# Two layers of message passing on one core: a prologue in two halves, and another order of the last steps of layer 0

## The chip, the core and the metric

The kernel runs on one core of one Trainium2 chip. The metric is the time of one launch in microseconds (us), taken on the device; three runs of the kernel before gave 2295.61, 2296.75 and 2296.79, a median of 2296.75. The core has five engines that run beside each other: TensorE (PE; PEld are its weight loads), VectorE (DVE), ScalarE (ACT), GpSimd (POOL) and SyncE (SP), and DMA queues that SP, ACT and POOL feed (SPq, ACTq, POOLq). Engines wait for each other by semaphores.

## The reference

N = 6250 nodes of D = 128 numbers and E = 106250 edges, sorted by destination.

```
h = relu(layernorm(x))
# layer 0: edge softmax per channel
msg = h[src] + edge_attr;  s = msg * beta
e = exp(s - segment_max(s, dst)[dst])
agg = segment_sum(msg * e / segment_sum(e)[dst], dst)
x = x + (agg @ H + bias + h)             # H from phm_rule and W
h = relu(layernorm(x))
# layer 1: graph attention, 4 heads of 32
Wx = h @ W.T;  logits = leaky_relu(a1.Wx[src] + a2.Wx[dst])
x = x + elu(segment_sum(softmax_per_dst(logits) * Wx[src], dst))
```

## The kernel before, in words

Edges are taken in groups of 512 (GE), four blocks of 128 (GB = 4); there are NG = 208 groups. Nodes are 49 tiles of 128 rows, in 13 batches of four tiles (the last has one). All inputs of x stay in SBUF as `nodes`.

Prologue. SyncE loads x in six parts of 512 KB and a small tail, then the weights. VectorE measures all 49 tiles (`statistics`, L869) and works out all norms at once (`norm_all_nodes`, L878 to L890: 18 small operations, each waiting for the one before). ScalarE loads the lists: src, dst and `prev` (dst shifted by one edge), eight of its eleven DMAs for the last two. When the norms are there, ScalarE makes h = relu(norm(x)) for the even batches (L673, a tile at a time) and VectorE for the odd ones (L912 four tiles, L916 the maximum of the batch). SyncE stores h batch by batch into `h_dram` (L381, L383), in order of batches. GpSimd adds h to `nodes` for even batches as they come (`even_residual`, L563), VectorE for odd ones after its list work (L941). List work: VectorE casts src (L904) and dst (L922), compares dst with prev to get run flags (L924, L925), TensorE transposes the tables (L1190), ScalarE copies them to `meta` (L687, L690), and SyncE brings the first lists to `meta_g` (L441 for src, L453 for the keys). Then follow packed offsets (L948 to L951), the matrix H (L957, L959) and constants on VectorE.

Layer 0 is one loop on each engine, `sweep_edges`, each engine with its own stages and lags; a stage at lag n handles group g - n in step g. GpSimd gathers four times 128 rows of h for each group (L582), waiting for the list, for h_stored, and for the lift of group g - 4. ScalarE lifts the rows to PSUM (`lift0`, L749, into row_psum), VectorE adds edge_attr (`add0`, L1017) and makes the one-hot (L1043), TensorE turns (`turn0`, L1238), VectorE scans for segment maxima in both directions and works out the drop between groups (`maxima0`, L994, L999, L1006, which counts `dropped`), TensorE turns back and subtracts (`unturn0`, L1245, L1249, into bank 2), ScalarE takes Exp twice (`weigh0`, L732, L735, L737), VectorE multiplies (`products0`, L1029), TensorE sums into `own_sums` (`sums0`, L1229), ScalarE merges that into the accumulator `acc` (`merge0`, L711 to L719). The loops run over their last steps in the same order as over the others; only before the last merge ScalarE loads the table of Ln (L752). After its last gather GpSimd adds the bias to all 13 batches of `nodes` (`add_bias`, L595).

Middle stage: ScalarE takes Ln and Exp (L760, L767), GpSimd multiplies (L606, L608), VectorE (L1059) and TensorE (L1272) finish layer 0, VectorE adds to `nodes` (L1068) where `bias_added` has come, measures and norms again. Layer 1 is a second loop of the same make; its last steps are written out by hand with `last(stage, back)`, which runs a stage for group NG - 1 - back, and use `spare_sums` in turn with `own_sums`. The order of instructions on each engine is the order of the program; there is no planner.

Of the kernel before, what the change touches and what calls it, by code (L numbers as in the profile page):

```python
# [70 lines left out]
def gnn_kernel(nc, x_in, src_in, dst_in, ea_in, rule_in, w0_in, bias_in, beta_in, w1_in, a_in, out):  # L71
# [31 lines left out]
    with ctx:  # L103
# [104 lines left out]
        row_psum = sums[:, 1, 0, :]  # L208
# [5 lines left out]
        own_sums, spare_sums = sums[:, 0, :, :], banks[:, 0:2, :]  # L214
# [40 lines left out]
        h_even = sem("h_even")  # L255
        h_odd = sem("h_odd")
        even_sum = sem("even_sum")
        odd_sum = sem("odd_sum")
        h_stored = sem("h_stored")
        bias_added = sem("bias_added")  # L260
# [64 lines left out]

        def extent(b):
            return (1, LAST) if b == NBAT - 1 else (GB, P)
# [16 lines left out]
        def _(sp):  # L344
# [12 lines left out]
            for i in range(PH):  # L357
# [16 lines left out]
            def store_h(b):  # L374
                t, r = extent(b)
                if b % 2:
                    sp.wait_ge(h_odd, b // 2 + 1)
                else:
                    sp.wait_ge(h_even, b // 2 + 1)
                if t == 1:  # L380
                    sp.dma_start(h_dram[b * GE:N, :], h_rows[0:r, b, 0, :]).then_inc(h_stored, 16)  # L381
                else:
                    sp.dma_start(h_dram[b * GE:(b + 1) * GE, :].rearrange("(t p) d -> p t d", p=P), h_rows[:, b, :, :]  # L383
                                 ).then_inc(h_stored, 16)

            straight(NBAT, [(0, store_h)])
# [131 lines left out]
        def _(pool):  # L518
# [39 lines left out]
            def even_residual(b):  # L558
                if b % 2 == 0:
                    t, r = extent(b)  # L560
                    pool.wait_ge(h_even, b // 2 + 1)
                    tiles = nodes[:, b * GB:b * GB + t, :]
                    pool.tensor_tensor(tiles, tiles, h_rows[:, b, 0:t, :], ALU.add).then_inc(even_sum, 1)  # L563

            straight(NBAT, [(0, even_residual)])
# [22 lines left out]
            pool.wait_ge(even_sum, (NBAT + 1) // 2)  # L588
            pool.wait_ge(odd_sum, NBAT // 2)
            pool.wait_ge(weights_in, 16 * W_DMA)  # L590

            def add_bias(b):
                t = 1 if b == NBAT - 1 else GB
                tiles = nodes[:, b * GB:b * GB + t, :]
                pool.tensor_tensor(tiles, tiles, bias_all[:, :].rearrange("p (a d) -> p a d", a=1).to_broadcast([P, t, D]),  # L595
                                   ALU.add).then_inc(bias_added, 1)

            straight(NBAT, [(0, add_bias)])
# [38 lines left out]
        def _(act):  # L637
# [7 lines left out]
            def load_list(flat, tile, done):  # L645
# [8 lines left out]
            act.wait_ge(x_loaded[4], 16)  # L654
            load_list(dst_in, dst_i, dst_in_sbuf)
            act.dma_start(prev_i[0:1, 0, 1:P], dst_in[0:P - 1].rearrange("(a e) -> a e", a=1)).then_inc(prev_in_sbuf, 16)
            act.dma_start(prev_i[1:P, 0, :], rows(dst_in, P - 1, P - 1)).then_inc(prev_in_sbuf, 16)
            act.dma_start(prev_i[:, 1:ct, :], dst_in[P * P - 1:ct * P * P - 1].rearrange("(t c e) -> c t e", c=P, e=P)
                          ).then_inc(prev_in_sbuf, 16)
            act.dma_start(prev_i[0:tail, ct, :], rows(dst_in, ct * P * P - 1, tail)).then_inc(prev_in_sbuf, 16)  # L660
            act.dma_start(prev_i[tail:tail + 1, ct, 0:E - FULL * P + 1],
                          dst_in[FULL * P - 1:E].rearrange("(a e) -> a e", a=1)).then_inc(prev_in_sbuf, 16)
# [3 lines left out]
            act.wait_ge(normed, 1)  # L666

            def even_h(b):
                if b % 2 == 0:
                    t, r = extent(b)  # L670
                    for i in range(t):
                        n = b * GB + i
                        ins = act.activation(h_rows[:, b, i, :], nodes[:, n, :], ACT.Relu,  # L673
                                             bias=norm[:, 1, n:n + 1], scale=norm[:, 0, n:n + 1])
                    ins.then_inc(h_even, 1)

            straight(NBAT, [(0, even_h)])
# [45 lines left out]
            act.wait_ge(blk_loaded, 16)  # L723

            act.wait_ge(h_stored, 16 * NBAT)
            act.wait_ge(even_sum, (NBAT + 1) // 2)

            def weigh0(g, s, use):
# [3 lines left out]
                act.activation(wgt[:, s % WGT, :, :], bank[2][:, :].rearrange("p (b d) -> p b d", b=GB), ACT.Exp)  # L732
                if later(g, 1):
                    act.wait_ge(L0["multiplied"], g)
                act.activation(wgt_psum, bank[2][:, :], ACT.Exp).then_inc(L0["weighed"], 1)  # L735
# [3 lines left out]
            def merge0(g, s, use):  # L739
                if isinstance(g, int) and g == 0:  # L740
                    act.wait_ge(odd_sum, NBAT // 2)
                merge(g, s, use, L0, None)
# [8 lines left out]
            sweep_edges(act, [(5, merge0), (0, lift0), (3, weigh0)], until=NG + 4)  # L751
# [39 lines left out]
            act.wait_ge(normed, 2)  # L791
# [61 lines left out]
        def _(dve):  # L853
# [21 lines left out]
            def norm_all_nodes():  # L875
                y, t, v = norm[:, 0, :], newton[:, :], spread_v[:, :]

                link(dve.tensor_tensor(t, stats[:, :, 1], stats[:, :, 4], ALU.subtract))  # L878
                link(dve.scalar_tensor_tensor(y, t, 0.25, t, ALU.mult, ALU.mult))
                link(dve.tensor_tensor(v, stats[:, :, 2], stats[:, :, 5], ALU.add))  # L880
                link(dve.scalar_tensor_tensor(v, v, 1.0 / D, y, ALU.mult, ALU.add))
                link(dve.tensor_tensor(mean_2[:, :], stats[:, :, 1], stats[:, :, 4], ALU.add))
# [7 lines left out]
                dve.scalar_tensor_tensor(norm[:, 1, :], mean_2[:, :], -0.5, y, ALU.mult, ALU.mult).then_inc(normed, 1)  # L890
# [3 lines left out]
            for k in range(LDX - 1):  # L894
# [6 lines left out]
            norm_all_nodes()  # L901

            dve.wait_ge(src_in_sbuf, 48)
# [281 lines left out]
        def _(pe):  # L1185
# [67 lines left out]
            def sums0(g, s, use):  # L1253
                segment_sums(g, s, L0)
# [137 lines left out]
```

## Time and profile before

| | |
|---|---|
| median of three runs | 2296.75 us |
| the profiled execution | 2297.38 us, its span 2295.6 us |
| PE, PEld busy | 88%, 79% |
| DVE busy | 87% |
| ACT busy | 59% |
| POOL busy | 72% |
| granted TensorE clock, mean | 0.945 |

Times in the views count from the start of the span. A busy share is an average over stages; the chain of waits goes back from the last instruction to what released each step, and tells which work ended last. "issue" in it is time in which an engine waited for nothing that the profile shows. Rows of a timeline give start, length, engine, line and operation, output<-input, shape and the number of instructions merged, and in brackets the idle time before with what ended it. A row of several instructions spans from the start of the first to the end of the last.

### The profile page before, as it was taken

What the parts mean: (1) busy time and instruction counts of PE and PEld (TensorE: products, weight loads), DVE (VectorE), ACT (ScalarE), POOL (GpSimd) and SP (SyncE); (2) the same over time, 40 slices, a digit from 0 to 9 for tenths busy, and PEclk for the clock granted to TensorE, in tenths of its full rate; (3) what the DMA queues carried; (4) which work ended last, traced back from release to release, by engine and by line L of the source; (5) the groups of instructions that cost most, each with busy time, mean ns of one, the idle gap of its engine ahead of it and who ended that gap; (6) DMA issues with size and microseconds to landing.
All of it is one profiled execution on the core that took longest, in us unless ns stands there. A gap on an engine that the chain in (4) does not pass through costs nothing.

```text
span 2295.6 us, 63252 instructions
## 1 busy us (share of the span) xinstructions
PE 2013.3 (88%) x15341; PEld 1806.1 (79%) x15342; DVE 1997.8 (87%) x3846; ACT 1361.5 (59%) x3479; POOL 1648.3 (72%) x1741
## 2 busy tenths in 40 slices
PE   1899999999999999998458999999999999999996
PEld 0778887888887888787458888888888888888885
DVE  7888989898989998999477888888888888888887
ACT  2566666666666666666544555555555555555555
POOL 4777777777777777777427777777777777777772
PEclk9999999999999999999677999999999999999998
DMA  7444454444444444443023333333333333333322
GB/s 209 116 132 135 131 136 131 126 131 135 131 136 131 136 129 128 131 136 99 1 62 61 61 58 59 58 59 59 59 59 59 58 59 59 58 59 58 59 60 67
DMA packets 338046, 214.22 MB, mean 93 GB/s; under 512 B 169981, under 2 KB 304502, under 8 KB 337990
## 3 DMA queue, kind: packets, MB, share of 16 engines
q0 software_dynamic: 53248, 112.57, 20.0%
q1 hardware_dynamic: 282190, 99.72, 17.3%
q10 hardware_dynamic: 2552, 1.28, 0.2%
q8 instruction: 24, 0.39, 0.1%
q14 instruction: 32, 0.26, 0.0%
HBM read 201.37 MB, written 10.29 MB: 92 GB/s over the span
## 4 chain that ended last, share of the span: by engine, by line
POOL 43%; issue 20%; DMA 14%; DVE 10%; PE 6%; ACT 4%; SPq 1%; POOLq 0%; ACTq 0%; DVEq 0%
POOL msg L618 23%; POOL ring_h L582 19%; DMA ring_h<-h_dram,meta_g 11%; PE sums L1229 3%; DVE sums L994 2%; DMA msg<-wx_dram,meta_g 2%; DVE seg_max L999 2%; ACT sums L749 2%; DVE onehot L978 1%; DVE prod L1129 1%; ACT acc L719 1%; PE banks L1238 1%; POOL ring_h L608 1%; PE banks L1245 1%; POOL diff L606 1%
## 5 line engine op out<-in xcount | busy, mean ns | idle before, releaser
L618 POOL DMA_INDIRECT msg<-wx_dram,meta_g x832 | 791.9, 952 | 293.5 <-issue 246.3
L582 POOL DMA_INDIRECT ring_h<-h_dram,meta_g x832 | 788.6, 948 | 260.8 <-issue 248.7
L1229 PE MATMUL sums<-onehot,prod 128*128 128x128 f32 x3312 | 688.2, 291 | 15.1 <-issue 6.1
L1229 PE MATMUL sums<-onehot,wgt 128*128 128x128 f32 x3312 | 674.1, 287 | 0.0
L1229 PEld LDWEIGHTS sums<-onehot,prod 128*128 128x128 f32 x3312 | 535.8, 204 | 47.7 <-issue 47.2
L1229 PEld LDWEIGHTS sums<-onehot,wgt 128*128 128x128 f32 x3312 | 536.7, 204 | 0.0
L719 ACT ACTIVATE acc<-sums 128x1022 f32 x412 | 422.0, 1024 | 0.2
L1238 PE MATMUL banks<-beta_ident,msg 128*128 128x128 f32 x1664 | 243.5, 290 | 91.3 <-DVE msg L1017 89.9
L749 ACT ACTIVATE sums<-ring_h 128x512 f32<-128x512 f32 x208 | 125.1, 602 | 321.7 <-DMA ring_h<-h_dram,meta_g 321.7
L1238 PEld LDWEIGHTS banks<-beta_ident,msg 128*128 128x128 f32 x1664 | 204.8, 194 | 119.7 <-issue 92.8
L1249 PEld LDWEIGHTS banks<-neg_ident,seg_max 128*128 128x128 f32 x1664 | 219.6, 192 | 100.5 <-issue 100.0
L994 DVE TENSOR_TENSOR_SCAN sums<-flags,seg_max,banks 4x512 f32<-4x512 bf16 x207 | 264.0, 1275 | 6.2 <-PE banks L1325 4.5
L994 DVE TENSOR_TENSOR_SCAN banks<-flags,seg_max,banks 128x512 f32<-128x512 bf16 x207 | 264.9, 1280 | 0.0
L999 DVE TENSOR_TENSOR_SCAN seg_max<-flags,banks 128x512 f32<-128x512 bf16 x208 | 253.9, 1220 | 7.2
L999 DVE TENSOR_TENSOR_SCAN seg_max<-flags,sums 4x512 f32<-4x512 bf16 x208 | 251.1, 1207 | 7.2
L711 ACT ACTIVATE carried<-acc,scale 128x2 f32 x414 | 121.5, 294 | 206.0 <-PE sums L1229 181.6
L1017 DVE TENSOR_TENSOR msg<-msg,sums 128x512 f32<-128x512 f32 x208 | 143.0, 687 | 89.8 <-ACT sums L749 82.7
L1249 PE MATMUL banks<-neg_ident,seg_max 128*128 128x128 f32 x1664 | 220.2, 275 | 0.0
L1316 PEld LDWEIGHTS banks<-window,onehotT 128*128 128x128 f32 x1664 | 211.6, 199 | 9.4 <-issue 8.1
L1245 PE MATMUL banks<-msg,beta_ident 128*128 128x512 f32 x416 | 214.8, 598 | 0.2 <-ACT sums L735 0.2
L1316 PE MATMUL banks<-window,onehotT 128*128 128x4 f32 x1664 | 205.8, 247 | 8.5 <-DMA window<-wx_dram 7.3
L808 ACT ACTIVATE sums<-logit_d 128x16 f32<-128x16 f32 x208 | 39.1, 188 | 256.3 <-DVE logit_d L1121 254.0
(162 smaller groups left out, 2806.3 us busy)
## 6 DMA issues: line engine op xcount, KB each, us to landing
msg<-in_edge_attr SPq DMA_DIRECT2D x207, 256.0 KB
flags<-flag_dram SPq DMA_DIRECT2D x52, 512.2 KB
ring_h<-h_dram,meta_g POOLq DMA_INDIRECT x832
msg<-wx_dram,meta_g POOLq DMA_INDIRECT x832
window<-wx_dram SPq DMA_DIRECT2D x832, 2.0 KB
wx_dram<-msg SPq DMA_DIRECT2D x13, 272.0 KB, 2.4
nodes<-in_x SPq DMA_DIRECT2D x6, 512.0 KB, 6.8
h_dram<-acc SPq DMA_DIRECT2D x12, 256.0 KB
```

The source lines that it names most:

```text
L582: pool.indirect_dma_start(hg[:, s % HRING, b, :], None, h_dram, bass.IndirectOffsetOnAxis(ap=meta_g[:, s, b:b + 1], axis=0)).then_inc(L0[" ...
L618: pool.indirect_dma_start(msg[:, s, b, :], None, wx_dram, bass.IndirectOffsetOnAxis(ap=meta_g[:, s, b:b + 1], axis=0)).then_inc(L1["gather ...
L719: act.activation(acc[:, :, bass.ds(node + 1, WIN - 1)], where[:, :, 1:WIN], ACT.Copy).then_inc(k["merged"], 1)
L749: act.activation(row_psum, ring_h[:, s % HRING, :], ACT.Copy).then_inc(L0["lifted"], 1)
L994: dve.tensor_tensor_scan(run, flag[:, 0:GE], data, before, ALU.add, ALU.max).then_inc(k["scanned"], 1)
L999: dve.tensor_tensor_scan(seg_max[0:n, par, ::-1], flag[:, GE:0:-1], run[:, ::-1], -BIG, ALU.add, ALU.max).then_inc(k["scanned"], 1)
L1017: dve.tensor_tensor(msg[:, s, :, 0:D], msg[:, s, :, 0:D], row_psum.rearrange("p (b d) -> p b d", b=GB), ALU.add).then_inc(L0["added"], 1)
L1229: ins = pe.matmul(where[:, j, bass.ds(off, P)], what[:, slot, b, :], onehot[:, s, b, :], start=(b == 0), stop=(b == GB - 1), skip_group_ch ...
L1238: ins = pe.matmul(bank[s % 2][:, b * P:(b + 1) * P], msg[:, s, b, 0:D], beta_ident[:, :], start=True, stop=True)
L1245: pe.matmul(bank[2][:, :].rearrange("p (b d) -> p b d", b=GB), beta_ident[:, :], msg[:, s, :, 0:D], start=True, stop=False, skip_group_che ...
L1249: ins = pe.matmul(bank[2][:, b * P:(b + 1) * P], seg_max[:, s % 2, b * P:(b + 1) * P], neg_ident[:, :], start=False, stop=(b == GB - 1), s ...
L1316: ins = pe.matmul(bank[1][:, b * H:(b + 1) * H], onehotT[:, s % 2, b * P:(b + 1) * P], window[:, s, b, :], start=True, stop=True)
```

## The change

- The two PSUM banks of `row_psum` and of the shift (the output of `unturn0`) change places; `spare_sums0` is banks 2 and 3. TensorE writes zeros to bank 3 once at the start.
- Prologue: `norm_nodes(lo, hi)` takes the place of `norm_all_nodes`. VectorE measures three parts of x (24 tiles, six batches), works out their norms, casts src, measures the rest and works out its norms. ScalarE makes h for batches 0 to 5, copies the src table, then makes h for 6, 8, 10 and 12; VectorE makes 7, 9 and 11. SyncE stores batches 0 to 5 in between the weights, the others in the order 7, 6, 9, 8, 11, 10, 12. The eight DMAs for dst and prev are issued by GpSimd, when the last full part of x has landed. GpSimd adds h to `nodes` for batches 0, 2 and 4, after VectorE's three batches; VectorE for the other ten.
- Bias: even batches on GpSimd, once all of layer 0's drops are made; odd ones on VectorE behind its last product.
- Last steps of layer 0: written out by hand on ScalarE, VectorE and TensorE, as in layer 1, with the spare banks for groups 204 and 206.

```diff
-        row_psum = sums[:, 1, 0, :]
+        shift_psum = sums[:, 1, 0, :]
+        row_psum = bank[2]
+        spare_sums0, spare_sums = banks[:, 2:4, :], banks[:, 0:2, :]
+        FRONT = 6
+        BY_DVE = (7, 9, 11)
+        BY_ACT = tuple(b for b in range(NBAT) if b not in BY_DVE)
+        POOL_SUMS = (0, 2, 4)
+        DVE_SUMS = tuple(b for b in range(NBAT) if b not in POOL_SUMS)
 # sync
             for i in range(PH):
+                store_h(i)
                 (rule_rep and w0_rep as before)
             for h in range(H):
+                if h < FRONT - PH:
+                    store_h(PH + h)
                 (a_col as before)
             (wx_dram pads as before)
-            straight(NBAT, [(0, store_h)])
+            for b in (7, 6, 9, 8, 11, 10, 12):
+                store_h(b)
 # gpsimd
-            straight(NBAT, [(0, even_residual)])
+            pool.wait_ge(x_loaded[5], 16)
+            pool.dma_start(dst_i[:, 0:ct, :], ...)        # 3 for dst_i, 5 for prev_i, which ACT issued before
...
+            pool.wait_ge(h_dve, len(BY_DVE))
+            for b in POOL_SUMS:
+                wait_row_batch(pool, b)
+                tiles = nodes[:, b * GB:(b + 1) * GB, :]
+                pool.tensor_tensor(tiles, tiles, h_rows[:, b, :, :], ALU.add).then_inc(pool_sum, 1)
             pool.wait_ge(h_stored, 16 * NBAT)
 (after the gathers of layer 0)
-            straight(NBAT, [(0, add_bias)])
+            pool.wait_ge(L0["dropped"], NG)
+            straight(NBAT, [(0, even_bias)])
 # scalar
+            act.wait_ge(normed, 1)
+            for b in range(FRONT):
+                h_by_act(b)
             (src table)
+            act.wait_ge(normed, 2)
+            for b in BY_ACT[FRONT:]:
+                h_by_act(b)
-            sweep_edges(act, [(5, merge0), (0, lift0), (3, weigh0)], until=NG + 4)
+            sweep_edges(act, [(5, merge0), (0, lift0), (3, weigh0)], until=NG - 1)
+            last(weigh0, 3)
+            last(merge0, 5)
+            last(weigh0, 2)
+            last(lift0, 0)
+            last(merge0, 4)
+            last(weigh0, 1)
+            last(merge0, 3, where=spare_sums0)
+            last(weigh0, 0)
+            last(merge0, 2)
+            last(merge0, 1, where=spare_sums0)
             act.activation(spare[:, :], spare[:, :], ACT.Ln)
             last(merge0, 0)
 # vector
+            (statistics of x_loaded 0 to 2)
+            dve.wait_ge(measured, FRONT)
+            norm_nodes(0, FRONT * GB)
+            dve.wait_ge(src_in_sbuf, 48)
+            dve.tensor_copy(src_f[:, :, :], src_i[:, :, :]).then_inc(src_rows, 1)
+            (statistics of the rest)
+            norm_nodes(FRONT * GB, NT)
+            (h for BY_DVE, list work, then)
+            for b in DVE_SUMS:
+                t, r = extent(b)
+                wait_row_batch(dve, b)
+                dve.tensor_tensor(tiles, tiles, h_rows[:, b, 0:t, :], ALU.add).then_inc(dve_sum, 1)
-            sweep_edges(dve, [(0, add0), (0, one_hot0), (3, products0), (1, maxima0)])
+            sweep_edges(dve, [(0, add0), (0, one_hot0), (3, products0), (1, maxima0)], until=NG - 1)
+            last(products0, 3)
+            last(maxima0, 1)
+            last(one_hot0, 0)
+            last(add0, 0)
+            last(products0, 2)
+            last(maxima0, 0)
+            last(products0, 1)
+            last(products0, 0)
+            (phm_neg, then)
+            straight(NBAT, [(0, odd_bias)])
 # tensor
+            pe.matmul(bank[3][:, :], zero_row[0:1, 0:P], zero_row[0:1, :], start=True, stop=True)
-            sweep_edges(pe, [(4, sums0), (0, turn0), (2, unturn0)])
+            sweep_edges(pe, [(4, sums0), (0, turn0), (2, unturn0)], until=NG - 1)
+            last(unturn0, 2)
+            last(sums0, 4)
+            last(turn0, 0)
+            last(unturn0, 1)
+            pe.wait_ge(L0["onehots"], NG)
+            pe.wait_ge(L0["added"], NG)
+            last(sums0, 3, where=spare_sums0, free=1)
+            last(sums0, 2, free=1)
+            last(unturn0, 0)
+            last(sums0, 1, where=spare_sums0, free=1)
+            last(sums0, 0, free=1)
```

## Rows read from the trace of the kernel before

**Rows 1.** The page's chain that ended last, by engine and line.
```profile
POOL msg L618 23%; POOL ring_h L582 19%; DMA ring_h<-h_dram,meta_g 11%; PE sums L1229 3%; DVE sums L994 2%; DMA msg<-wx_dram,meta_g 2%; DVE seg_max L999 2%; ACT sums L749 2%; DVE onehot L978 1%; DVE prod L1129 1%; ACT acc L719 1%; PE banks L1238 1%; POOL ring_h L608 1%; PE banks L1245 1%; POOL diff L606 1%
```

**Rows 2.** Stretches: length, busy of PE, PEld, DVE, ACT, POOL, clock, DMA.
```profile
200.00:500.00 300.00, 279.08 (x2045) 242.16 (x2046) 270.70 (x362) 196.97 (x483) 226.56 (x242) 1.00 0.47 132
```

**Rows 3.** Timeline of GpSimd: first and last gathers of layer 0, bias additions.
```profile
43.27 3.89 POOL L582 DMA_INDIRECT ring_h<-h_dram,meta_g  x1 [7.51 <-DMA meta_g<-meta]
47.47 1.44 POOL L582 DMA_INDIRECT ring_h<-h_dram,meta_g  x1 [0.30 <-issue]
49.20 0.99 POOL L582 DMA_INDIRECT ring_h<-h_dram,meta_g  x1 [0.30 <-issue]
...
1084.18 0.94 POOL L582 DMA_INDIRECT ring_h<-h_dram,meta_g  x1 [0.30 <-issue]
1085.16 15.08 POOL L595 TENSOR_TENSOR nodes<-nodes,bias_all 128x512 f32<-128x512 f32 x13
```

**Rows 4.** Timelines of TensorE, VectorE and ScalarE behind the last gather.
```profile
1084.91 1.05 PE L1249 MATMUL banks<-neg_ident,seg_max 128*128 128x128 f32 x8
...
1086.68 13.16 DVE L1006 SCALAR_TENSOR_TENSOR drop<-seg_max,flags 128x1 f32<-128x1 f32 x1
...
1101.56 1.27 DVE L994 TENSOR_TENSOR_SCAN banks<-flags,seg_max,banks 128x512 f32<-128x512 bf16 x1
...
1105.21 0.60 ACT L732 ACTIVATE wgt<-banks 128x512 f32<-128x512 f32 x1 [13.77 <-PE banks L1249]
...
1117.04 1.28 ACT L752 ACT_TABLE_LOAD   x1
...
1122.25 2.19 ACT L760 ACTIVATE onehot<-acc 128x512 f32<-128x512 f32 x4
```

**Rows 5.** The chain in order of time, behind the last gather: start, length, what.
```profile
1105.17 1.80 PE sums L1229 x16
1107.15 0.30 ACT carried L711
1107.85 1.03 ACT acc L719
...
1117.16 3.17 PE sums L1229 x16
```

**Rows 6.** Timeline of the middle stage.
```profile
1148.44 1.09 POOL L606 TENSOR_TENSOR diff<-acc,ring_h 128x512 f32<-128x512 f32 x1
1148.51 0.69 DVE L1059 SCALAR_TENSOR_TENSOR ring_h<-banks,ring_h 128x512 f32<-128x512 f32 x1
```

**Rows 7.** Timeline of the prologue.
```profile
6.63 3.43 DVE L869 BATCH_NORM_STATS2 stats<-nodes 128x6 f32<-128x128 f32 x16
...
9.57 0.23 ACTq L648 DMA_DIRECT2D fin<-in_src  x1
...
17.78 0.25 DVE L878 TENSOR_TENSOR newton<-stats 128x49 f32<-128x49 f32 x1
...
22.00 0.21 DVE L890 SCALAR_TENSOR_TENSOR norm<-mean,norm 128x49 f32<-128x49 f32 x1
...
24.70 9.70 ACT L673 ACTIVATE acc<-nodes,norm 128x128 f32<-128x128 f32 x25
...
28.13 3.00 DVE L912 TENSOR_SCALAR diff<-nodes,norm 128x128 f32<-128x128 f32 x4
...
36.22 1.11 DVE L912 TENSOR_SCALAR diff<-nodes,norm 128x128 f32<-128x128 f32 x4
...
37.71 0.62 DVE L922 CAST ring_h<-pos 128x896 f32<-128x896 int32 x1
...
42.49 3.68 DVE L941 TENSOR_TENSOR nodes<-nodes,acc 128x512 f32<-128x512 f32 x6
```

**Rows 8.** The line of the loads of x: from issue to landing.
```profile
DMA to landing us min/median/max: 4.0/6.8/7.4
```

**Rows 9.** The chain in order of time, in the prologue.
```profile
38.69 3.71 DMA meta_g<-meta
```

More of the change, by code:

```diff
@@ L213, in gnn_kernel @@
         bank = [banks[:, i, :] for i in range(4)]
-        own_sums, spare_sums = sums[:, 0, :, :], banks[:, 0:2, :]
+        row_psum = bank[2]
+        own_sums = sums[:, 0, :, :]
+        spare_sums0, spare_sums = banks[:, 2:4, :], banks[:, 0:2, :]
         iota_psum = bank[3][:, 0:P]
@@ L324, in sweep_edges, with wait_row_batch, add_bias @@
             sweep(eng, NG, RING, stages, reach=RING, until=until)
+        FRONT = 6
[3 more added lines that the diff above has]
+        DVE_SUMS = tuple(b for b in range(NBAT) if b not in POOL_SUMS)
+        def wait_row_batch(eng, b):
+            if b in BY_DVE:
+                eng.wait_ge(h_dve, BY_DVE.index(b) + 1)
+            else:
+                eng.wait_ge(h_act, BY_ACT.index(b) + 1)
+        def add_bias(eng, b, done):
+            t = 1 if b == NBAT - 1 else GB
+            tiles = nodes[:, b * GB:b * GB + t, :]
+            eng.tensor_tensor(tiles, tiles, bias_all[:, :].rearrange("p (a d) -> p a d", a=1).to_broadcast([P, t, D]),
+                              ALU.add).then_inc(done, 1)
         def extent(b):
@@ L653, in _, with h_by_act @@
             load_list(src_in, src_i, src_in_sbuf)
[L654 to L662, printed above, removed]
             act.wait_ge(const_ready, 1)
             act.activation(spare[:, :], spare[:, :], ACT.Exp, scale=0.0)
[L666 to L677, printed above, removed]
+            def h_by_act(b):
+                t, r = extent(b)
+                for i in range(t):
+                    n = b * GB + i
+                    ins = act.activation(h_rows[:, b, i, :], nodes[:, n, :], ACT.Relu,
+                                         bias=norm[:, 1, n:n + 1], scale=norm[:, 0, n:n + 1])
+                ins.then_inc(h_act, 1)
             meta_t = meta[:, :, :].rearrange("p (t g) k -> p t g k", t=CT)
@@ L723, in _ @@
             act.wait_ge(blk_loaded, 16)
+            act.wait_ge(key_out, len(TABLE_BANKS))
             act.wait_ge(h_stored, 16 * NBAT)
-            act.wait_ge(even_sum, (NBAT + 1) // 2)
+            act.wait_ge(pool_sum, len(POOL_SUMS))
             def weigh0(g, s, use):
@@ L889, in norm_all_nodes @@
                     link(dve.scalar_tensor_tensor(y, t, 1.5, y, ALU.add, ALU.mult))
-                dve.scalar_tensor_tensor(norm[:, 1, :], mean_2[:, :], -0.5, y, ALU.mult, ALU.mult).then_inc(normed, 1)
+                dve.scalar_tensor_tensor(norm[:, 1, lo:hi], m, -0.5, y, ALU.mult, ALU.mult).then_inc(normed, 1)
             per = (NT - 1) // (LDX - 1) // GB
-            for k in range(LDX - 1):
+            front_parts = FRONT // per
+            for k in range(front_parts):
+                dve.wait_ge(x_loaded[k], 16)
+                for b in range(k * per, (k + 1) * per):
+                    statistics(b)
+            dve.wait_ge(measured, FRONT)
+            norm_nodes(0, FRONT * GB)
+            dve.wait_ge(src_in_sbuf, 48)
+            dve.tensor_copy(src_f[:, :, :], src_i[:, :, :]).then_inc(src_rows, 1)
+            for k in range(front_parts, LDX - 1):
                 dve.wait_ge(x_loaded[k], 16)
@@ L1244, in unturn0 @@
                     pe.wait_ge(L0["weighed"], g)
-                pe.matmul(bank[2][:, :].rearrange("p (b d) -> p b d", b=GB), beta_ident[:, :], msg[:, s, :, 0:D],
+                pe.matmul(shift_psum.rearrange("p (b d) -> p b d", b=GB), beta_ident[:, :], msg[:, s, :, 0:D],
                           start=True, stop=False, skip_group_check=True)
```

134 lines of the change are left out of this document (67 added, 67 removed).

## The prediction

> **What bounds the kernel now.** I read the page's chain of waits first, then the table of stretches, then the timeline of each engine where the chain is not plain gather issue. The chain [rows 1] spends most of its time on GpSimd and on "issue", and its two largest lines are the two gathers, L582 in layer 0 and L618 in layer 1. In the middle of layer 0 [rows 2] VectorE is busy 270.70 of 300 us and TensorE 279.08, so neither is full. The timeline of GpSimd shows what sets the pace [rows 3]: the third gather of layer 0 starts at 49.20 and the last of 832 at 1084.18, so 829 steps take 1034.98 us, 1.248 us each. That is the 0.94 us of one gather and the 0.30 us ahead of it, without one wait. Four gathers make a group, 4.99 us; the 208 groups of layer 0 are a rigid block, and all other engines follow it. So the kernel is: a prologue until that stream runs freely, the block, the last steps of layer 0 (the drain), a middle stage, layer 1 of the same kind, the end. The diff touches the prologue and the drain, and swaps two PSUM banks in the block. Layer 1 and what follows is not edited and moves as a whole.
>
> The drain is where the trace has a surprise. GpSimd's thirteen bias additions start at 1085.16, right after its last gather, and last 15.08 us [rows 3]. VectorE's small operation L1006, which reads seg_max and flags in SBUF, starts at 1086.68 and takes 13.16 us [rows 4] for one column; it ends as the additions end. The row of ScalarE's log, the first after the last merge, stands at 1122.25. So some 13 us of the 37 us from the last gather to the log are one instruction kept out by another engine.
> The Trainium skill (SBUF — State Buffer, "SBUF: two separate sides") says that a VectorE op with two SBUF inputs and a GpSimd op share a port pair as an exclusive lock, which whichever starts first holds "for the whole instruction". By that rule L1006 would wait for one addition, a little over 1 us, and taking the additions away would give 1 us; the trace gives 13.16 us, all that was left of them, and the measurement decides.
>
> **Drain, edit by edit.** (1) The bias additions: seven stay on GpSimd but wait for the last `dropped`, which is behind the last L1006; six go to VectorE behind its last product. So the stall of 13 us goes. What VectorE still does beside GpSimd's seven additions are products, which read PSUM and SBUF. Such an operation isn't slowed: in the middle stage L1059 (banks and ring_h) takes 0.69 us while GpSimd's L606 runs [rows 6]. VectorE's phm_neg and its six additions (0.61 us each by the six sums of L941 in 3.68 us [rows 7]) may wait for GpSimd's seven, about 7.7 us (15.08 less six of 1.23).
> (2) The order of the last steps, and the spare banks for two of the last four sums. I lay it out with durations of the drain: a weigh 1.2 us, its second Exp done after 1.1 (L732 starts at 1105.21 [rows 4]); a merge 1.73 from L711 to the end of L719, the sixteen matmuls of a sum 1.80 [rows 5]; a turn 1.1, an unturn 1.9, two scans with their drop 2.8 (each scan some 1.25 [rows 4]); a lift or product 0.6; 0.1 to 0.2 us to be released. The last instruction that both orders share is unturn of group 204, which ends at 1085.96 (L1249 [rows 4]). Then: weigh 204 frees its bank at 87.1 (I leave out the 1000); unturn 205 87.2 to 89.1; merge 202 87.2 to 88.9; weigh 205 89.2 to 90.4; lift 207 90.3 to 90.9. On VectorE: product 204 87.2 to 87.9, scans of 206 to 90.6, one-hot 207 to 91.2, add 207 to 91.9, product 205 to 92.4. Turn 207 ends at 93.1, unturn 206 at 94.9; scans of 207 93.2 to 96.0. TensorE goes on: sum 204 (spare) to 96.6, sum 205 to 98.4, unturn 207 to 100.3, sum 206 (spare) to 102.1. ScalarE: weigh 206 95.0 to 96.2, merge 204 to 98.5, weigh 207 100.4 to 101.6, merge 205 to 103.3, which frees sum 207, 103.4 to 105.2. Merge 206 ends at 104.9, the Ln table and its operation take 1.5 more (table 1.28 [rows 4]) to 106.4, the last merge 106.5 to 108.2. The log starts at 1108.2 and not at 1122.25: a gain of 14.0 us. The bias work: GpSimd from 96.0 to 103.7, VectorE from there to 107.6; nobody needs it before the middle stage's first finish. From below: with TensorE at its lower clock a sum takes 3.17 us [rows 5], and two of them on the path would leave 11. From above: 15.5, if the releases overlap better.
>
> **Block.** Swapping the banks of the lift and of the shift changes no wait and no size. VectorE has 0.49 us of slack in each group of 4.99 [rows 2] and GpSimd does not touch PSUM: 0 us. Its bounds are 0 and, if an access got slower by more than that slack, 208 times the excess.
>
> **Prologue, edit by edit.** (3) VectorE: the statistics of the first 24 tiles end at 10.06 (16 tiles in 3.43 from 6.63 [rows 7]). A norm is 18 small operations, 17.78 to 22.21 for 49 columns; half the columns make it about 4.0, so the first is ready at 14.1. Then comes the cast of src. Its loads are issued until 9.80, and a load of x beside them needs 4.0 to 7.4 us to land [rows 8], so it lands between 14.1 (no wait) and 17.2; I take 15.3. Cast 0.6, statistics of 24 tiles 4.9, the last tile 0.3, norm 4.0: 25.1. Three batches on VectorE at 1.49 us (36.22 to 37.71 [rows 7]): 29.6.
> (4) ScalarE has no dst issues any more, so its table load lies before 11.3. Its 25 tiles took 9.70 us, 0.388 each: six batches 14.1 to 23.4, the src table 0.9 to 24.4, thirteen tiles from 25.1 to 30.2. Before, the last batch was ready at 37.8 (VectorE's); now at 30.2.
> (5) SyncE stores in the new order; the last store is issued at 30.5, the list of the first gathers at 30.9. That took 3.71 us to land before [rows 9]: 34.6, and the first gather started 0.87 us behind the landing: 35.4 against 43.27, with weights long issued between the stores.
> (6) The dst and prev lists, eight DMAs of GpSimd from 13.9 on. The trace has no plain DMA issued there. Nearest row: a gather of 128 rows, 0.94 us, 7.4 ns a row. The lists have 830 rows each; 1660 rows and eight gaps of 0.30 give 14.6 us, until 28.5. Lower end: eight short issues like SyncE's, a few us. Upper end: twice the row's price, 27 us, until 41. I take 14.6, hidden: GpSimd waits until 29.6 for VectorE's three batches anyway. The Trainium skill (DMA: Bandwidth & Descriptors, "Latency and other measured facts") puts GpSimd's emission at about 1 us; eight of these would end at 22, hidden too; no row here shows it.
> (7) GpSimd's three residual sums at 1.22 us, like the additions of [rows 3] (15.08 us for twelve and a quarter): 29.6 to 33.3, before the first gather. They hit VectorE's list work now: its batch work of 28.13 to 36.22 took 8.1 us for two batches where free it is 3.0 [rows 7], a loss of 5.1 beside some four and a half additions (5.5 us); so beside sums VectorE loses nine tenths of their time, 3.4 us. Its stretch from the cast of dst to the end of the residual sums was 37.71 to 46.17 [rows 7], 8.46 us; four more sums add 2.45. So its end is 29.6 + 3.4 + 8.5 + 2.5 = 44.0.
> (8) That decides when the stream is free. Before, the first gather took 3.89 us [rows 3] and ended at 47.16, 1.0 us behind the last residual sum; it was shut out. Now the sums run about 37.8 to 44.0 and the gather starts at 35.4. In the gap until 37.8, where VectorE works in small pieces and waits for TensorE's transpose, I let one gather pass; the second ends at about 45.0 (before: 48.91, of which half a us was contention that stays). Gain 3.9 less some rest: 3.7 us. If none passes, the first ends at 45.0 against 47.16: gain 2.2. If two pass: 5.2. If nothing shuts gathers out: 7.9 and the 3.5 us of before's losses, 11. If src lands at 17.2 all is 1.9 later: gain 1.8. The middle work of VectorE (weights, packed offsets) keeps its 6 us and is ready at 50, before the first rows are lifted; a group's lift may lag its gather by some 12 us (three groups less landing) before the ring of four stops GpSimd.
> TensorE's extra matmul at the start costs nothing, which has no work before the src table.
>
> **Sum.** 14.0 + 3.7 = 17.7 us off the profiled execution of 2297.4 (span 2295.6) is 2279.7. The median of the three timed runs is 2296.75, 0.6 below it: **2279.0**.
>
> **Rivals.** A, forecast: gathers shut out by VectorE's ten sums, drain as laid out; gain 14 to 20.
> B: the gathers pass between or beside the sums; the first starts at 35.4 and the stream is freed early. Gain 14 + 8 = 22: 2275, at most 25. For it: before, the shut-out gather was only one, and later gathers beside VectorE's SBUF operations took 1.44 and 0.99. Against: 3.89 beside six sums in a row.
> C: the prologue gives nothing back or costs a few us, since lists come late from GpSimd (each us that its issues end beyond about 28 delays dst, and with it keys and sums) or sums shut out more. The upper price of (6) has dst landing at 43, keys and sums 11 us behind that, the free stream at 55 and not 48.9: loss 6, gain in all 8: 2289. For: it is a new place for eight DMAs.
> D: the drain stalls again in another place: the six additions of VectorE behind GpSimd's seven, or GpSimd's on a last product; then up to 7.7 us come back and the gain is 10: 2287. Against: rows 6.
> E, slower than before: plain DMAs on GpSimd are paid by the row at a multiple of the gather's price. With X the end of issue, dst lands at X + 2, and VectorE's 14.3 us (3.4 + 8.5 + 2.4) and a gather follow: the second gather ends at X + 17.3. The 14 us of the drain are used up at 48.9 + 14 = 62.9, so X = 45.6: 31.7 us for 1660 rows, 19 ns a row against 7.4 measured. At 25 ns a row the time is 2307. Only such a price decides; the block's bank swap would need 0.57 us more in each of VectorE's groups (0.49 slack and 17.7/208).
>
> **Chances.** A 0.60, B 0.14, C 0.13, D 0.07, E with no change 0.06. A measurement of this kernel tells about 0.2% (4.6 us) from no change: faster 0.94, same 0.02, slower 0.04. A alone is 2276 to 2283. The range takes in most of B, the near half of C and part of D: **2272 to 2286**.
>
> **What would show it.** In the timeline after: L1006's operation of group 205 at a fraction of a microsecond; the log 22 to 24 us behind the last gather (37 to 38 before); bias additions on GpSimd behind the last drop; VectorE's products there still near 0.69. In the prologue: first norm at 14, last batch of h near 30, the first gather near 35 and a long one (several us) beside L941's ten sums, the stream free 3 to 5 us earlier; GpSimd's list issues ending before 29. Layer 0 again 1.248 us a gather. It would be wrong if the new list issues run past 30 us, if a gather of the block waits, or if the merges of 204 to 207 stand further apart than 2 to 5 us.

## The result: 5.0 us faster, 12.8 us short of the forecast

The changed kernel takes 2291.76 us (median of 15 runs, 2290.99 to 2294.32), the kernel before beside it 2296.79 us (15 runs, 2295.51 to 2298.24). The ratio is 0.9979, 95% interval [0.9971, 0.9987]: a gain of 5.0 us where 17.7 were forecast. 2291.76 lies above the range, nearest to rival C, whose reason (late lists) isn't in the trace. Some executions named further down, of the kernel before as well, took 3.3 to 3.5 ms at a granted clock of 0.79 and not 0.95; from these only the lengths of gathers are read, beside each other.

The profiled execution after has a span of 2292.5 us and took 2294.32, 2.6 above its median. Cut at the same events, the two profiled executions compare so (us; from the timelines of GpSimd and the rows of ScalarE's log):

| stretch | before | after | gain |
|---|---|---|---|
| start to third gather of layer 0 | 49.20 | 44.92 | 4.3 |
| from there to the last gather of layer 0 | 1034.98 | 1041.26 | -6.3 |
| to the log (the drain) | 38.07 | 23.83 | 14.2 |
| to the first gather of layer 1 | 79.23 | 78.34 | 0.9 |
| gathers of layer 1 | 1044.32 | 1051.18 | -6.9 |
| from there to the end | 49.8 | 53.0 | -3.2 |

The two stretches that were forecast to gain, the first and the drain, do gain, 18.5 together. Both blocks of gathers lose, 13.2 together; 829 steps of layer 0 take 1.2560 us each where they took 1.2485. (Most of the 3.2 us at the end belong to this one execution: with the same last part, the runs below have 49.6 to 51.4.)

One gather's own rows show it. First the two gather lines of the kernel before, then of the kernel after: minimum, median and maximum of one, in ns, then the start of the first and of the last; "issue" is the idle time ahead of them, in us, and how often.

```profile
L582 POOL DMA_INDIRECT ring_h<-h_dram,meta_g x832: 940/944/3889, 43.3 to 1084.2; - x167
L618 POOL DMA_INDIRECT msg<-wx_dram,meta_g x832: 940/944/1074, 1201.5 to 2245.8; - x167
```

```profile
L616 POOL DMA_INDIRECT ring_h<-h_dram,meta_g x832: 947/952/5810, 37.5 to 1086.2; - x167
...
  issue: 247.8, 813
...
L651 POOL DMA_INDIRECT msg<-wx_dram,meta_g x832: 947/952/1092, 1188.3 to 2239.5; - x167
...
  issue: 246.3, 808
```

The median went from 944 to 952 ns, and the minimum moved with it, from 940 to 947: all gathers are longer, not some of them. The gap ahead of each, "issue", stayed (before 248.7 and 246.3 us over the two lines). Seventeen gathers of layer 0 have their gap put down to ScalarE, 5.2 us in all (before fifteen, 4.6 us); that is the same 0.3 us each. Eight ns over 1664 gathers are 13.3 us. So behind the first ones no gather of layer 0 waits; the middle of layer 0 looks like [rows 2] with a little less done in it:

```profile
200.00:500.00 300.00, 277.65 (x2031) 240.49 (x2031) 269.04 (x360) 196.29 (x480) 227.16 (x240) 1.00 0.47 131
```

GpSimd's prologue and first gathers in the timeline after, which answer to [rows 3]:

```profile
14.04 1.05 POOL L583 DMA_DIRECT2D pos<-in_dst  x1 [4.74 <-DMA nodes<-in_x]
15.09 0.61 POOL L584 DMA_DIRECT2D pos<-in_dst  x1
...
18.83 0.51 POOL L592 DMA_DIRECT2D elu_e<-in_dst  x1
30.80 5.24 POOL L599 TENSOR_TENSOR nodes<-nodes,acc 128x512 f32<-128x512 f32 x3 [11.46 <-DVE acc L958]
37.47 1.03 POOL L616 DMA_INDIRECT ring_h<-h_dram,meta_g  x1 [1.42 <-DMA meta_g<-meta]
38.81 5.81 POOL L616 DMA_INDIRECT ring_h<-h_dram,meta_g  x1 [0.30 <-issue]
44.92 0.95 POOL L616 DMA_INDIRECT ring_h<-h_dram,meta_g  x1 [0.30 <-issue]
```

The eight list DMAs end at 19.34, GpSimd then idles 11.46 us, one gather passes, the second takes 5.81 us beside VectorE's ten sums, and the third is free at 44.92. VectorE and ScalarE in the same stretch, as [rows 7]:

```profile
13.82 0.18 DVE L927 SCALAR_TENSOR_TENSOR norm<-mean,norm 128x24 f32<-128x24 f32 x1
16.66 0.63 DVE L939 CAST hT<-fin 128x896 f32<-128x896 int32 x1 [2.66 <-DMA fin<-in_src]
...
25.95 0.18 DVE L927 SCALAR_TENSOR_TENSOR norm<-mean,norm 128x25 f32<-128x25 f32 x1
...
30.63 0.62 DVE L962 CAST ring_h<-pos 128x896 f32<-128x896 int32 x1
...
38.08 5.68 DVE L982 TENSOR_TENSOR nodes<-nodes,acc 128x512 f32<-128x512 f32 x10
```

```profile
14.04 9.34 ACT L694 ACTIVATE acc<-nodes,norm 128x128 f32<-128x128 f32 x24 [2.72 <-DVE norm L927]
...
26.17 5.11 ACT L694 ACTIVATE acc<-nodes,norm 128x128 f32<-128x128 f32 x13 [1.94 <-DVE norm L927]
```

The first norm is there at 14.00, `src` lands at 16.66, the second norm is there at 26.13, ScalarE's last tile at 31.28. And the drain, the timelines of all engines behind the last gather, against [rows 4]:

```profile
1086.18 0.95 POOL L616 DMA_INDIRECT ring_h<-h_dram,meta_g  x1 [0.30 <-issue]
...
1088.69 0.22 DVE L1044 SCALAR_TENSOR_TENSOR drop<-seg_max,flags 128x1 f32<-128x1 f32 x1
...
1098.00 8.27 POOL L343 TENSOR_TENSOR nodes<-nodes,bias_all 128x512 f32<-128x512 f32 x7 [10.87 <-DVE drop L1044]
...
1098.57 0.69 DVE L1067 TENSOR_TENSOR prod<-sums,msg 128x512 f32<-128x512 f32 x1 [0.74 <-PE banks L1285]
...
1104.19 5.03 DVE L343 TENSOR_TENSOR nodes<-nodes,bias_all 128x512 f32<-128x512 f32 x6
...
1110.01 2.19 ACT L796 ACTIVATE onehot<-acc 128x512 f32<-128x512 f32 x4
```

The operation that took 13.16 us takes 0.22. The bias additions stand behind the last drop; the product beside them takes its usual 0.69. TensorE's clock is part of this gain. Before, TensorE had no matmul while VectorE stood still, and the granted clock fell:

```profile
1090.00:1100.00 10.00, 0.00 (x0) 0.00 (x0) 10.00 (x2) 1.35 (x4) 10.00 (x10) 0.53 0.00 0
...
1100.50 2.08 PE L1238 MATMUL banks<-beta_ident,msg 128*128 128x128 f32 x8 [12.75 <-DVE msg L1017]
```

The first of these is a stretch, in the columns of [rows 2]. The last turn, at a clock of 0.50, took 2.08 us, and the last sum, over which the clock was 0.61 in the mean, 3.17 [rows 5]. After, the clock is 1.00 from 1086 to 1110; that turn takes 1.16.

### The profile page after: what moved, and what is told of

It is laid out like the page before. It is cut to its first block, busy times and chain, and to the rows that moved or that the text cites. A ratio compares the mean times of both kernels' runs of the same rounds, so it can differ in the third digit from the quotient of the medians.

```text
span 2292.5 us, 63277 instructions
## 1 busy us (share of the span) xinstructions
PE 2013.6 (88%) x15342; PEld 1804.4 (79%) x15343; DVE 1987.7 (87%) x3859; ACT 1365.1 (60%) x3491; POOL 1658.6 (72%) x1739
## 4 chain that ended last, share of the span: by engine, by line
POOL 47%; issue 21%; DMA 13%; DVE 8%; PE 5%; ACT 3%; SPq 1%; POOLq 1%; ACTq 0%; DVEq 0%
POOL msg L651 25%; POOL ring_h L616 21%; DMA ring_h<-h_dram,meta_g 9%; DMA msg<-wx_dram,meta_g 3%; DVE sums L1032 2%; DVE seg_max L1037 2%; PE sums L1285 2%; ACT banks L775 1%; DVE onehot L1016 1%; DVE prod L1184 1%; POOL ring_h L641 1%; POOL diff L639 1%; ACT acc L744 0%; PE banks L1294 0%; SPq L505 0%
## 5 line engine op out<-in xcount | busy, mean ns | idle before, releaser
L651 POOL DMA_INDIRECT msg<-wx_dram,meta_g x832 | 798.8, 960 | 292.6 <-issue 246.3
L1285 PE MATMUL sums<-onehot,prod 128*128 128x128 f32 x3296 | 680.2, 290 | 14.7 <-issue 6.6
L1285 PE MATMUL sums<-onehot,wgt 128*128 128x128 f32 x3296 | 667.3, 286 | 0.0
L1285 PEld LDWEIGHTS sums<-onehot,prod 128*128 128x128 f32 x3296 | 529.4, 202 | 47.3 <-issue 46.8
L775 ACT ACTIVATE banks<-ring_h 128x512 f32<-128x512 f32 x208 | 125.2, 602 | 323.3 <-DMA ring_h<-h_dram,meta_g 322.5
L1305 PEld LDWEIGHTS sums<-neg_ident,seg_max 128*128 128x128 f32 x1664 | 220.2, 193 | 100.4 <-issue 100.4
L1055 DVE TENSOR_TENSOR msg<-msg,banks 128x512 f32<-128x512 f32 x208 | 143.0, 687 | 93.3 <-ACT banks L775 86.8
L1305 PE MATMUL sums<-neg_ident,seg_max 128*128 128x128 f32 x1664 | 220.7, 276 | 0.0
L1301 PE MATMUL sums<-msg,beta_ident 128*128 128x512 f32 x416 | 215.0, 599 | 1.3 <-ACT sums L761 1.2
```

The costliest lines, as they stand in the source:

```text
L651: pool.indirect_dma_start(msg[:, s, b, :], None, wx_dram, bass.IndirectOffsetOnAxis(ap=meta_g[:, s, b:b + 1], axis=0)).then_inc(L1["gather ...
L775: act.activation(row_psum, ring_h[:, s % HRING, :], ACT.Copy).then_inc(L0["lifted"], 1)
L1055: dve.tensor_tensor(msg[:, s, :, 0:D], msg[:, s, :, 0:D], row_psum.rearrange("p (b d) -> p b d", b=GB), ALU.add).then_inc(L0["added"], 1)
L1285: ins = pe.matmul(where[:, j, bass.ds(off, P)], what[:, slot, b, :], onehot[:, s, b, :], start=(b == 0), stop=(b == GB - 1), skip_group_ch ...
L1301: pe.matmul(shift_psum.rearrange("p (b d) -> p b d", b=GB), beta_ident[:, :], msg[:, s, :, 0:D], start=True, stop=False, skip_group_check= ...
L1305: ins = pe.matmul(shift_psum[:, b * P:(b + 1) * P], seg_max[:, s % 2, b * P:(b + 1) * P], neg_ident[:, :], start=False, stop=(b == GB - 1) ...
```

## Experiments

The question was which edit makes every gather 8 ns longer. Theory: the plain DMAs that the change issues on GpSimd. Rivals: another edit of the diff (the drain's, the bank swap), and later, for what it is about such a DMA, three readings. Ratios, and times where a difference is named, are against the kernel before beside them (medians of 2296.45 to 2297.08 us). A label that ends in _2 is the same kernel again.

**1. The lists' DMAs on SyncE** (lists_on_sp, again as lists_on_sp_2): the changed kernel with one block moved.

```diff
-pool.wait_ge(x_loaded[5], 16)
-pool.dma_start(dst_i[:, 0:ct, :], ...)   # and seven more
+sp.wait_ge(pads_in, 3)
+sp.dma_start(dst_i[:, 0:ct, :], ...)     # and seven more
```

> The changed kernel with its eight plain DMAs for dst and prev taken from GpSimd and issued by SyncE behind beta; nothing else. Theory 1 (a plain DMA on GpSimd makes every later gather longer): the median gather is 0.944 us again and not 0.952, both blocks of 832 gathers give back 6 to 7 us each, and the time is 2277 to 2281, about 12 us below the changed kernel's 2291.8. Theory 2 (the gather is longer for another reason, as the PSUM swap, one more semaphore, or code placed elsewhere): gathers stay at 0.952 and the time stays within 2 us of 2291.8.

> The changed kernel with its eight plain DMAs issued by SyncE instead of GpSimd, once more, on another chip. Theory 1 (one plain DMA on GpSimd lengthens every later gather): median gather 0.944 us, time 2277 to 2281. Theory 2 (another cause): 0.952 and 2290 to 2294.

Measured: 2279.86 us (2278.97 to 2283.03), ratio 0.9931 [0.9914, 0.9947]. The gathers are back at 944 ns in both layers (at the clock of 0.79 947, the same as in drain_only there):

```profile
L615 POOL DMA_INDIRECT ring_h<-h_dram,meta_g x832: 940/944/3742, 41.4 to 1082.1; - x167
L650 POOL DMA_INDIRECT msg<-wx_dram,meta_g x832: 940/944/1094, 1184.3 to 2227.3; - x167
```

The third gather starts at 47.18 and not 44.92: SyncE has more to issue, the list of the first gathers leaves at 36.33 and not 32.79, and the first gather, at 41.38, no longer comes ahead of VectorE's ten sums (from 38.44). Even so, 12 us come back. Blocks 1034.94 and 1043.02. All that is left of the change (bank swap, order, norms) costs the block nothing.

**2. The lists' DMAs on GpSimd in the kernel before** (lists_on_pool): the same block put ahead of its residual sums, ScalarE's issues taken out.

> The kernel before with one move alone: the eight plain DMAs for dst and prev are issued by GpSimd behind the fifth part of x. Theory 1: gathers go from 0.944 to 0.952 in both layers and the time from 2296.8 to about 2309 (13 us for 1664 gathers), less what ScalarE's earlier start gives in the prologue (0 to 4). Theory 2: gathers stay at 0.944 and the time is 2293 to 2297.

Measured, at the clock of 0.79 alone: gathers of 952 ns in both layers, against 947 in lists_on_sp and drain_only beside it. The edit brings the longer gathers by itself. The price in time that was expected, about 13 us, was not measured: there 3358.41 us stand against 3360.83, and gathers of layer 0 wait 422 us for ScalarE, so that their own length no longer sets the time.

**3. One plain DMA of 32 bytes** (one_plain, again as one_plain_2), the kernel before with:

```diff
+pool.dma_start(tiny[:, :], a_in[0:8]...).then_inc(tiny_in, 16)
+pool.wait_ge(tiny_in, 16)
 def even_residual(b):
```

> The kernel before with one plain DMA of 32 bytes on GpSimd ahead of its residual sums, into a tile that nobody reads. Theory 1 in the form that any plain DMA does it: gathers at 0.952 as behind eight. In the form that it grows with their number: 0.945. Theory 2: 0.944.

> The kernel before with one plain DMA of 32 bytes on GpSimd, once more. Theory 1: 0.952 a gather, 13 us more: 2308 to 2312. Theory 2: no change, 2296 to 2298.

Measured: 2309.08 us (2308.19 to 2309.86), ratio 1.0052 [1.0035, 1.0069]: 12.3 us for one DMA whose own issue takes 0.74. One of 32 bytes does what eight of up to 384 KB do.

```profile
L560 POOL DMA_DIRECT2D tiny<-in_L_gnn_a x1: 737/737/737, 9.2 to 9.2; - x1
L587 POOL DMA_INDIRECT ring_h<-h_dram,meta_g x832: 947/952/3799, 43.3 to 1090.4; - x167
L623 POOL DMA_INDIRECT msg<-wx_dram,meta_g x832: 947/952/1097, 1207.4 to 2257.9; - x167
```

Its third gather starts at 49.19, where it was before; block 1041.20 (before 1034.98), layer 1's 1050.57 (1044.32).

**4. The drain alone** (drain_only, again as drain_only_2): the kernel before with the bias additions, the last steps and the banks of the change, its prologue untouched.

> The kernel before with the bias split, the last steps of layer 0 by hand and the PSUM swap; the prologue is the one of before. Theory 1: gathers at 0.944, the log 24 us behind the last gather and not 38, so a time of 2282 to 2284. Theory 2, if the swap or the additional semaphore lengthens gathers: 0.952 and 2295 to 2297.

> The kernel before with the bias split, the last steps by hand and the PSUM swap, once more. Theory 1: gathers at 0.944, log 24 us behind the last gather, 2282 to 2284. Theory 2: 0.952, 2295 to 2297.

Measured: 2283.19 us (2281.71 to 2283.95), ratio 0.9942 [0.9925, 0.9958]: 13.6 us. Its log stands 23.84 us behind its last gather, its gathers take 944 ns, its block 1035.0 us: the bank swap costs nothing.

**5. The bias additions alone** (bias_only): as 4, without the new order of the last steps and without spare banks; `dve.wait_ge(bias_added, b + 1)` becomes a wait on the even or the odd half.

> The kernel before with the bias split and its wait for the last drop, and nothing else: steps, banks and prologue as before. Theory 1 (the stall of L1006 is nearly all of the drain's gain): add 207 comes some 12 us sooner, and time is 2284 to 2286, the order of the last steps being worth 1 to 2 us of the 13.5. Rival (the order by hand matters as much): 2289 or more.

Measured: 2283.78 us (2283.18 to 2284.44), ratio 0.9942 [0.9927, 0.9957]. The gain is 12.7 us. The log stands 23.93 us behind the last gather, 14.1 less than before. So the stall taken away gives nearly all of the drain's gain, and the order written out by hand is worth 0.1 us by these rows, where 1 to 2 were expected. By the times it is 0.9 us (13.6 less 12.7), which intervals of some 3 us to either side don't tell from nothing.

```profile
1089.18 0.69 DVE L1023 TENSOR_TENSOR msg<-msg,sums 128x512 f32<-128x512 f32 x1 [1.56 <-ACT sums L755]
...
1089.92 1.16 PE L1253 MATMUL banks<-beta_ident,msg 128*128 128x128 f32 x8 [1.46 <-DVE msg L1023]
```

VectorE's add of the last group, at 1099.77 before, comes 11.3 us sooner, counted from the last gather. The other 2.9 us lie between this add and the log, 22.5 us before and 19.6 here, in the same order: TensorE stays at a clock of 1.00, and in the chain of waits the last turn takes 1.16 us and not 2.08, the first two matmuls of the unturn behind it 0.86 and not 1.71, the last sum 2.04 and not 3.17. These three make the 2.9.

**6. The plain DMA between the layers** (plain_between): the line of 3, ahead of the gathers of layer 1. At first I had two readings: each gather issued behind a plain DMA is longer (2302 to 2304 us, layer 1 alone), or the program as such is (2308 to 2310 us).

> The kernel before with one plain DMA of 32 bytes on GpSimd between the two layers. If a plain DMA leaves a state behind it: gathers of layer 0 at 0.944, of layer 1 at 0.952, time 2302 to 2304. If it is a property of the program that holds such an instruction: both at 0.952, 2308 to 2310.

Measured: 2298.6 us (2297.09 to 2300.75), ratio 1.0010 [1.0001, 1.0019]. Both readings fall: 945 ns in both layers, as in bias_only and one_gather beside it. The minimum in layer 1 is 942 where it is 940 in layer 0, and the time is 2.2 us above the kernel before; where these come from isn't shown.

```profile
L584 POOL DMA_INDIRECT ring_h<-h_dram,meta_g x832: 940/945/3841, 43.5 to 1084.8; - x167
L620 POOL DMA_INDIRECT msg<-wx_dram,meta_g x832: 942/945/1095, 1202.3 to 2247.1; - x167
L624 POOL DMA_DIRECT2D tiny<-in_L_gnn_a x1: 587/587/587, 1161.9 to 1161.9; - x1
```

**7. An extra gather in the same place** (one_gather), to see whether any early DMA of GpSimd does it:

```diff
+pool.indirect_dma_start(tiny[:, :], None, x_in, IndirectOffsetOnAxis(ap=iota_i[:, 0:1], axis=0)).then_inc(tiny_in, 16)
+pool.wait_ge(tiny_in, 16)
```

> The kernel before with one more indirect DMA of 128 rows in the prologue of GpSimd. If only a plain DMA does it: 0.944. If any additional DMA shifts something in the queue: 0.952.

Measured, one run: 2299.28 us, 2.8 above the kernel before, and 945 ns. It doesn't lengthen them.

```profile
L587 POOL DMA_INDIRECT ring_h<-h_dram,meta_g x832: 940/945/3867, 43.8 to 1084.7; - x167
```

**8. Gather first, then the plain DMA** (gather_then_plain, again as gather_then_plain_2): the lines of 7 and behind them that of 3, in the kernel before.

> The kernel before, with one extra gather of 128 rows as GpSimd's first DMA in its prologue and right behind it the single plain DMA of 32 bytes that one_plain_2 had there alone. If what counts is which kind of DMA GpSimd issues first, the gathers of both layers keep a median of 944 or 945 ns and the time is that of the kernel before, 2296 to 2299 us. If any plain DMA ahead of the layers' gathers does it, whatever went before, they take 952 ns, the block of layer 0 is 1041.2 us instead of 1035, and the time is 2307 to 2310 us.

> The kernel gather_then_plain again, for its time: by the order of the DMAs 2296 to 2299 us and gathers of 944 or 945 ns; without an effect of the order 2307 to 2310 us and 952 ns.

Measured: 2299.34 us (2298.67 to 2302.87), ratio 1.0013 [1.0004, 1.0022], as 7 without the plain DMA. It is 2.3 us above the kernel before where 3, with the plain DMA alone, is 12.3 above it. One more DMA in front, and a wait for its landing, take away four fifths of the loss; the minimum is 944, not 940, and not 947:

```profile
L561 POOL DMA_INDIRECT tiny<-in_x,iota_i x1: 1137/1137/1137, 9.5 to 9.5; - x1
L563 POOL DMA_DIRECT2D dot<-in_L_gnn_a x1: 564/564/564, 16.4 to 16.4; - x1
L590 POOL DMA_INDIRECT ring_h<-h_dram,meta_g x832: 944/945/3848, 43.5 to 1085.5; - x167
L626 POOL DMA_INDIRECT msg<-wx_dram,meta_g x832: 944/945/1078, 1201.7 to 2246.4; - x167
```

**9. The changed kernel with a gather first** (gather_first, again as gather_first_2): the two lines of 7 ahead of its eight plain DMAs, nothing else.

> The changed kernel, with one extra gather of 128 rows (its rows are used by nothing) ahead of the eight plain DMAs on GpSimd; everything else stays. If the kind of the first DMA counts, the gathers go back to 944 ns at the median, both layers lose some 6 us each, and the time is 2278 to 2282 us, since the prologue's GpSimd work has room for one more gather. If plain DMAs ahead of the layers' gathers count in any order, the gathers stay at 952 ns and the time is 2290 to 2294 us.

> The kernel gather_first again, on another chip: on the one of its first run the kernel before took 3427.6 us, so only the lengths of its gathers (945 ns at the median) could be read. By the order of the DMAs it takes 2278 to 2282 us, with the third gather at 44 to 46 us and both layers' gathers at 944 or 945 ns. If plain DMAs ahead of the layers' gathers count in any order, 952 ns and 2290 to 2294 us.

Measured: 2279.44 us (2278.71 to 2280.27), ratio 0.9924 [0.991, 0.9937], 0.4 us from the forecast for the change itself. (gather_first, at the clock of 0.79, has 945 ns.) Third gather at 45.24, log 23.95 us behind the last gather:

```profile
L584 POOL DMA_INDIRECT tiny<-in_x,iota_i x1: 1121/1121/1121, 9.5 to 9.5; - x1
L587 POOL DMA_DIRECT2D pos<-in_dst x1: 893/893/893, 16.2 to 16.2; - x1
...
L620 POOL DMA_INDIRECT ring_h<-h_dram,meta_g x832: 940/944/5854, 37.7 to 1080.3; - x167
L655 POOL DMA_INDIRECT msg<-wx_dram,meta_g x832: 940/944/1097, 1182.2 to 2226.7; - x167
```

**10. Two versions meant to be faster.** best: the lists on SyncE, the twelve small loads of weights on ScalarE behind its part of h, GpSimd's residual sums 0 to 3 early and 4 to 6 behind VectorE's part, six sums on VectorE and not ten. best2: the kernel of 9 with those sums.

> The changed kernel with the lists issued by SyncE, the twelve small weight DMAs moved from SyncE to ScalarE behind its last batch of h, GpSimd's residual sums of batches 0 to 3 as soon as they are there and 4 to 6 behind VectorE's three batches, so that VectorE has six sums and not ten. Theory (gathers of 0.944, and the first ones shut out by VectorE's sums): third gather at 43 instead of 44.9 in the changed kernel and 47.2 with lists on SyncE alone; time 2275 to 2277. Rival (sums shut nothing out, the lists' landing decides): 2278 to 2280.

> gather_first, with the residual sums of batches 0 to 3 on GpSimd ahead of its wait for VectorE's part of h and 4 to 6 behind it, and six sums instead of ten on VectorE. The lists stay on GpSimd and the weights on SyncE as in the change. If the extra gather keeps the later ones at 944 ns, the third gather starts at 43.5 to 45 and the time is 2276 to 2279 us, level with the version called best (2278.0) within 1.5 us. If not, the time is 2288 to 2292 us.

Measured: best 2277.98 us (2274.77 to 2278.79), ratio 0.9916 [0.9902, 0.9929], the lowest of all, though not told apart from 9 by these intervals. It misses the 2275 to 2277 us that were expected by 1 us, and its third gather starts at 44.78 where 43 was expected. best2 was measured at the clock of 0.79 alone, so its forecast of the time stays open; its gathers take 944 ns there. Its third gather starts at 46.10 where 43.5 to 45 was expected: its early sums, from 21.20 to 26.12, run into VectorE's second norm, and VectorE's last batch ends at 34.3 and not at 31.0 as in gather_first beside it.

## Why the prediction was wrong

The step that failed is **"Block. ... 0 us"**, with the sentence that "layer 1 and what follows is not edited and moves as a whole". I priced the bank swap in the block, and for the plain DMAs of step (6) only their own issue time. Runs 1 to 3 show that they lengthen each of the 1664 gathers from 944 to 952 ns. That is 13.2 us of the two blocks; 17.7 less 13.2 is 4.5, and 5.0 was measured. Run 9 takes this term away, with one gather added, and lands 0.4 us from the forecast; run 1 lands 0.9 from it. So there is no second error of size in the total, though some smaller ones cancel in it.

Point by point:
- (1), the stall: right. Log 24.0 us behind the last gather laid out, 23.83 measured; gain 14.0 forecast, 14.2 measured, and 12.7 and 13.6 in the times of bias_only and drain_only_2.
- (2), the order: the sum was right, but the credit isn't the order's (0.1 us by rows, run 5). My layout of the new order, with sums at full clock, was compared with the trace of before, stall and slow matmuls included, and never with the old order without the stall. I saw the sum of 3.17 us only as a danger to the new order; that the stall itself had brought the low clock, and that 2.9 of the 14.1 us go with it, I didn't see. Rival D fell: the product beside GpSimd's additions takes 0.69 us.
- (3) to (5): `src` landed at 16.66, where I took 15.3 of a range of 14.1 to 17.2. It moved all behind it by 1.0 to 2.1 us: second norm 26.1 (25.1), end of h 31.3 (30.2), the list's issue 32.79 (30.9), first gather 37.47 (35.4).
- (6), the price of issue: 5.3 us for eight, 0.51 to 1.05 each, where I took 14.6 by rows; hidden either way, as said. The Trainium skill (DMA: Bandwidth & Descriptors, "Latency and other measured facts") puts GpSimd's overhead of emission at about 1 us to the first byte. Taken as a price for each issue, as I took it, that was the nearer of the two; the rows after have 0.51 to 1.05 us. Rival E had the right edit and the wrong mechanism: a price paid at once and by the row, where it is paid later by each gather.
- (7) and (8): end of VectorE's sums 43.8 (44.0), one gather passes, the second ends at 44.6 (45.0), gain 4.3 (3.7). The ten sums decide, as I said, but that their end came out so near is partly luck. The late `src` moved VectorE's batches too, which end at 30.7 (29.6), and by my own chain that makes the sums late. It was made good by two terms that I had too large: the list work lost 2.7 us beside GpSimd's sums (3.4), and the ten sums took 5.7 (6.1). GpSimd's three sums took 5.2 us in their turn (3.7) and end at 36.0 (33.3); that was hidden, since the first gather waited for its list until 37.5. B and C fell.
- "Layer 0 again 1.248 us a gather" was named as the sign to look for; it is where the trace disagreed. "A gather of the block waits" wasn't the form that it took: none waits, each is longer.

What stays open: why a plain DMA has this effect, and whether it is its being GpSimd's first that counts. All three programs in which a plain DMA comes first (the change, lists_on_pool, one_plain) have 952 ns, at either clock; the ten with none, with one behind gathers or with a gather ahead of it have 944 to 947. But the gather ahead, with the wait for its landing, also makes the plain DMA late. It starts at 9.24, 12.26 and 14.04 us in the three, and at 16.18 and 16.41 in runs 9 and 8. No run has a gather ahead of a plain DMA that starts before 14 us, or a plain DMA that comes first but after 16 us, so order and time of issue aren't told apart. The work inside such an instruction has no rows. That the place of the code in memory, which each of these edits also moves, plays a part isn't excluded; it would have to follow the order of DMAs in all thirteen programs.

## What to carry to other kernels

Where one kind of instruction sets the pace and occurs 1664 times, compare its minimum and median in ns before anything else: 8 ns here took back 13.2 of the 18.5 us that two stages had gained, and no wait or idle row showed it. Price work that is newly put on the engine of that stream twice, for its own time and for what it does to the stream behind it, and allow that term more than zero in the range. If GpSimd feeds a long stream of gathers, keep plain DMAs on other queues, or let a gather be its first DMA. And before crediting a reordering, lay out the old order with the stall removed as well, at the clock that TensorE has without the stall.

## What the runs showed of the hardware

- A plain DMA as GpSimd's first, issued at 9 to 14 us: later gathers of 128 rows 952 ns at the median, not 944; 12.3 us here for 32 bytes. Behind 832 gathers (run 6) or behind one, at 16.4 us (run 8): 945 ns, and 2.2 and 2.3 us.
- Issue of a plain DMA on GpSimd: 0.51 to 1.05 us; of a gather of 128 rows, 0.94, or 1.12 to 1.14 where it is the first.
- Shutting out goes both ways and outlasts one instruction: VectorE's one-column operation sat out some eleven additions of GpSimd (13.16 us, [rows 4]); one gather took 5.81 us beside ten VectorE sums (5.68 us) and 3.89 beside six (3.68). VectorE reading PSUM and SBUF isn't held (0.69 us beside additions).
- A stop of TensorE is paid again behind it: with no matmul from 1090 to 1100 the granted clock was 0.53 in that stretch and 0.50 until 1104, and a turn of eight matmuls took 2.08 us, not 1.16.
